# Cross-attention maxima over pairs of 512-key chunks, in bursts of one 512-column round

## The reference

```
x = x + cross_attention(layernorm(x), ctx)      # q: 512 x 512, ctx: 8192 x 512, 16 heads of 32, RoPE
x = x + self_attention(layernorm(x))            # causal, 512 x 512
x = x + experts(layernorm(x))                   # top 4 of 32 experts, and a shared one

cross_attention:  q = x @ W_q + b_q;  k, v = split(y @ W_kv + b_kv);  q, k = rope(q), rope(k)
                  softmax(q @ k.T / sqrt(32)) @ v, then @ W_o + b_o
```

## Time and profile before

| | |
|---|---|
| median of three runs | 1490.36 us |
| profiled execution | 1485.93 us, span 1484.6 us |
| busy, share of the span | PE 95%, DVE 78%, ACT 69%, POOL 42% |
| granted TensorE clock, mean | 0.988 |
| first score burst, last score burst | at 72.7 us, at 582.8 us |
| second, third, fourth stage begin | 590.5, 1147, 1265 us |

### The profile page before, as it was taken

One profiled execution on the slowest core, in us unless ns is written; L12 is line 12 of the kernel. 1 busy time (PEld: TensorE's weight loads), 2 busy tenths in 40 slices (PEclk: granted clock), 3 DMA queues, 4 the chain that ended last, 5 costly groups with the idle time before them and its releaser, 6 DMA issues.

```text
span 1484.6 us, 29090 instructions
## 1 busy us (share of the span) xinstructions
PE 1406.3 (95%) x11020; PEld 854.0 (58%) x11020; DVE 1150.7 (78%) x2814; ACT 1023.8 (69%) x1318; POOL 626.9 (42%) x426
## 2 busy tenths in 40 slices
PE   7999999999999976999999999999999899899993
PEld 5866666666666643555555555555555766644441
DVE  6888777877877775899999999998988866533334
ACT  5577777777777775988899888988998456301221
POOL 0199787877787982132122223220000311054541
PEclk9999999999999999999999999999999999999997
DMA  5464344444333326855545544556551240357994
GB/s 197 136 238 157 128 143 162 151 141 144 128 128 128 129 74 191 219 131 129 121 118 128 127 117 119 132 119 173 130 125 48 98 170 2 148 191 280 410 407 174
DMA packets 94592, 229.74 MB, mean 155 GB/s; under 512 B 12737, under 2 KB 13130, under 8 KB 91638
## 3 DMA queue, kind: packets, MB, share of 16 engines
q1 hardware_dynamic: 88288, 218.37, 46.8%
q0 software_dynamic: 5600, 8.42, 1.6%
q10 hardware_dynamic: 566, 1.09, 0.2%
HBM read 171.15 MB, written 64.91 MB: 159 GB/s over the span
## 4 chain that ended last, share of the span: by engine, by line
PE 68%; POOL 13%; DVE 7%; ACT 4%; issue 4%; DMA 3%; SPq 1%; POOLq 0%; ACTq 0%; DVEq 0%
PE PS L817 18%; PE PS L841 16%; PE PS L340 6%; PE PS L344 6%; PE PS L299 4%; PE PS L1648 4%; POOL kr L633 3%; POOL W_ L631 3%; POOL kr L630 3%; POOL R L622 2%; PE PS L1665 2%; PE PS L849 2%; PE PS L1607 2%; DVE rel L607 2%; POOL kl L648 1%
## 5 line engine op out<-in xcount | busy, mean ns | idle before, releaser
L875 ACT ACTIVATE P<-PS 128x1024 f32<-128x1024 f32 x512 | 487.2, 1027 | 63.6 <-PE PS L817 58.8
L607 DVE CUSTOM_DVE_ANT_0 rel<-PS,rel 128x256 f32<-128x256 f32 x1024 | 363.2, 420 | 106.2 <-PE PS L299 104.3
L935 DVE TENSOR_TENSOR W_<-W_,P 128x2048 f32<-128x2048 f32 x108 | 254.8, 2425 | 8.4 <-ACT P L875 8.1
L841 PE MATMUL PS<-P,qe 128*32 128x256 f32 (+1 forms) x4032 | 255.8, 386 | 0.0
L935 DVE TENSOR_TENSOR acc<-acc,P 128x2048 f32<-128x2048 f32 x108 | 245.3, 2335 | 12.8 <-ACT P L875 12.5
L841 PEld LDWEIGHTS PS<-P,qe 128*32 128x32 f32 x4032 | 115.5, 109 | 115.8 <-issue 54.5
L459 ACT ACTIVATE rel<-PS 128x1024 f32<-128x1024 f32 x128 | 131.6, 1028 | 71.8 <-PE PS L299 71.7
L344 PE MATMUL PS<-Wh,R 128*128 128x512 f32 x512 | 179.3, 413 | 0.0
L340 PE MATMUL PS<-R,Wh 128*128 128x512 f32 x512 | 175.8, 414 | 3.1 <-ACT kr L426 3.1
L465 ACT ACTIVATE rel<-PS 128x1024 f32<-128x1024 f32 x128 | 131.5, 1028 | 45.0 <-PE PS L299 44.4
L299 PE MATMUL PS<-khd,qh 32*128 32x256 f32 x2048 | 130.0, 327 | 23.8 <-DVE mpart L607 11.9
(11 more groups left out here) (304 smaller groups left out, 2061.8 us busy)
## 6 DMA issues: line engine op xcount, KB each, us to landing
khd<-kscr SPq DMA_DIRECT2D x129, 256.0 KB, 4.2
y<-in_y SPq DMA_DIRECT2D x16, 1024.0 KB, 5.2
vscr<-W_ SPq DMA_DIRECT2D x16, 1024.0 KB, 4.9
kscr<-khd SPq DMA_DIRECT2D x16, 1024.0 KB, 6.9
kscr<-kl SPq DMA_DIRECT2D x16, 1024.0 KB, 5.0
qe<-vscr SPq DMA_DIRECT2D x64, 256.0 KB, 2.7
kl<-kscr SPq DMA_DIRECT2D x63, 256.0 KB, 4.3
Wp<-in_w_e SPq DMA_DIRECT2D x6, 1536.0 KB
```

What stands on the lines that cost most here:

```text
L607: last = dve.tensor_tensor_reduce(out=rel[i][:, j, t, :], in0=PS[:, 2 * b + j, t * 256:(t + 1) * 256], in1=rel[i][:, j, t, :], scale=1.0, ...
L841: ins = pe.matmul(PS[32 * hd:32 * hd + 32, 6, cols], vt[n % 3][:, j, 32 * hd:32 * hd + 32], P[z % 4][:, hd, cols], start=kt == 0, stop=kt ...
L875: act.activation(P[s % 4][:, 2 * pr:2 * pr + 2, :], PS[:, 2 * b:2 * b + 2, :], ACT.Exp, scale=SCALE).then_inc(exp_done, 1)
L935: dve.tensor_tensor(a[:, :, :], a[:, :, :], P[s % 4][:, :, :], ALU.add).then_inc(summed, 1)
```

## The change

In the first stage a chunk is no longer folded in itself. Key i of chunk 2m is paired with key i of chunk 2m+1, `kd` = key of 2m − key of 2m+1 (512 columns), and `b` is chunk 2m+1. There are 8 pairs of chunks, and for each 4 groups, 4 query tiles and 2 pairs of heads: 256 half steps. `half_step(k)` is one burst of four matmuls of 512 columns, in the order `kh`, `kd`, `kh`, `kd`: the `b` scores of half step k into banks 0 and 1 or 2 and 3, and the differences of half step k+1 into banks 4 and 5. ACT's relu for k+1 follows; DVE's two instructions of 512 columns for k need the relu taken one half step before. PE waits at half step k for that relu of k (`relued`, k+1) and for DVE to have finished k−2 (`max_taken`, k−1). One `kd` and one `kh[1]` serve all pairs, so POOL and ACT wait before they overwrite a group (`last_b`), and ACT waits before it overwrites `kr[0]` until POOL has made the difference from it.

The table `SCORES` starts at slot 216 (before: 170), advances by 5 and 6 in turn, by 5 from k = 192 on, and skips to 936, 1128 and 1320 for the pairs 4, 5 and 6, whose keys are ready then. The last half step has slot 1640, 104 after the last unit; before it was 1540 at the latest. 21 of the half steps come after the last projection matmul. `ROPE`, `KEY_HIGH`, `Y_HIGH`, `KEY_LOW`, `Y_LOW` stay where they were.

In the third stage the units with `u % 3 == 2` begin with a mask matmul of 384 columns for each head (zeros, mask, mask), and the scores of both tiles are added to it. ACT prepares the wider mask with three instructions in place of one.

```diff
-Y_HIGH, Y_LOW, KEY_LOW, SCORES_1, SCORES_2, MAXIMA = {}, {}, {}, {}, {}, {}
+Y_HIGH, Y_LOW, KEY_LOW, SCORES, MAXIMA = {}, {}, {}, {}, {}
...
+KEYS_READY = {(c_, g_): slot_ + 8 for slot_, (c_, g_) in KEY_HIGH.items()}
+slot_ = 0
+for k_ in range(-1, HALF_STEPS):
+    m_, g_, t_, h_ = step_of(min(k_ + 1, HALF_STEPS - 1))
+    slot_ = max(slot_ + (6 if k_ % 2 and k_ < 6 * 32 else 5), KEYS_READY[2 * m_ + 1, g_])
+    SCORES[slot_] = k_
...
-    def score_pairs(n, which, left, right):
-        c, g, qp = n // 8, n % 8 // 2, n % 2
-        for t in range(2):
-            qt = 2 * qp + t
-            for hd in range(4):
-                rows = slice(32 * hd, 32 * hd + 32)
-                keys = slice(256, 512) if hd // 2 == which else slice(512, 768)
-                o = PS[:, 2 * (left if hd // 2 == which else right) + hd % 2, t * 256:(t + 1) * 256]
-                last = pe.matmul(o, qh[rows, g, qt * 128:(qt + 1) * 128], khd[c % 2][rows, g, keys],
+    def half_step(k):
+
+        for j in range(2):
+            if k >= 0:
+                m, g, qt, which = step_of(k)
+                rows = slice(32 * (2 * which + j), 32 * (2 * which + j) + 32)
+                last = pe.matmul(PS[:, 2 * (k % 2) + j, :], qh[rows, g, qt * 128:(qt + 1) * 128], kh[1][rows, g, :],
+                                 start=True, stop=True)
+            if k + 1 < HALF_STEPS:
+                m, g, qt, which = step_of(k + 1)
+                rows = slice(32 * (2 * which + j), 32 * (2 * which + j) + 32)
+                last = pe.matmul(PS[:, 4 + j, :], qh[rows, g, qt * 128:(qt + 1) * 128], kd[rows, g, :],
                                  start=True, stop=True)
...
+            if k < 0:
+                pe.wait_ge(q_out_ps, 4)
             else:
-                pe.wait_ge(q_out_ps, 4)
-            score_pairs(n, 0, n % 3, (n + 1) % 3).then_inc(sc1_made, 1)
...
+                pe.wait_ge(relued, k + 1)
+            if k > 1:
+                pe.wait_ge(max_taken, k - 1)
+            half_step(k).then_inc(sc_made, 1)
...
+        if slot in SCORES and SCORES[slot] + 1 < HALF_STEPS:
+            k = SCORES[slot] + 1
+            act.wait_ge(sc_made, scored(k - 1))
+            if k > 1:
+                act.wait_ge(max_taken, k - 1)
+            act.activation(rel[k % 2][:, :, :], PS[:, 4:6, :], ACT.Relu).then_inc(relued, 1)
...
-    def larger(n, hp, i, b):
-        c, g, qp = n // 8, n % 8 // 2, n % 2
+    def larger(k):
+        m, g, qt, which = step_of(k)
         for j in range(2):
-            for t in range(2):
-                last = dve.tensor_tensor_reduce(
-                    out=rel[i][:, j, t, :], in0=PS[:, 2 * b + j, t * 256:(t + 1) * 256], in1=rel[i][:, j, t, :],
-                    scale=1.0, scalar=NEG, op0=ALU.add, op1=ALU.max,
-                    accum_out=mpart[:, 4 * (2 * hp + j) + g, 2 * qp + t, c:c + 1])
+            last = dve.tensor_tensor_reduce(
+                out=rel[k % 2][:, j, :], in0=PS[:, 2 * (k % 2) + j, :], in1=rel[k % 2][:, j, :],
+                scale=1.0, scalar=NEG, op0=ALU.add, op1=ALU.max, accum_out=mpart[:, 4 * (2 * which + j) + g, qt, m:m + 1])
...
-                if c > 1 and g == 0:
-                    pool.wait_ge(sc2_made, 8 * (c - 1))
-                pool.wait_ge(k_turned, turned(c, g, 3))
-                pool.tensor_tensor(khd[c % 2][:, g, 512:768], x[:, 0:256], x[:, 256:512],
-                                   ALU.subtract).then_inc(k_turned, 1)
+                if c % 2:
+                    if c > 1:
+                        pool.wait_ge(sc_made, scored(last_b(c - 2, g)))
...
+                    pool.wait_ge(k_turned, turned(c, g, 3))
+                    pool.tensor_tensor(kd[:, g, :], kr[0][:, g, :], x, ALU.subtract).then_inc(k_turned, 1)
...
+        if u % 3 == 2:
+            for hd in (2 * hp, 2 * hp + 1):
+                pe.matmul(PS[:, 2 + hd, 0:384], idr[:, :], mkr[:, :], start=True, stop=False)
+            for qt, off in TILES[2]:
+                w = 128 * (qt + 1)
+                for hd in (2 * hp, 2 * hp + 1):
+                    ins = pe.matmul(PS[:, 2 + hd, off:off + w], qk[0][ROWS[hd], g, qt * 128:(qt + 1) * 128],
+                                    qk[1][ROWS[hd], g, 0:w], start=False, stop=qt == 0)
```

More of the change, by code:

```diff
@@ L60, with step_of @@
     KEY_LOW[12 * (first_key(c_) + 8 + {0: 5, 1: 6, 14: 1, 15: 1}.get(c_, late_)) + 5] = c_
[L61 to L69, removed]
+    if c_ == NCH - 2:
+        FIRST_KEYS = max(KEY_LOW) + 30
+HALF_STEPS = 2 * 16 * (NCH // 2)
+def step_of(k):
+    return k // 32, k % 32 // 8, k % 8 // 2, k % 2
+KEYS_READY = {(c_, g_): slot_ + 8 for slot_, (c_, g_) in KEY_HIGH.items()}
[4 more added lines that the diff above has]
+    SCORES[slot_] = k_
+    if k_ >= 7 * 32 and k_ % 8 == 7:
+        MAXIMA[slot_ + 2] = k_ % 32 // 8
 SECOND_KEYS = 12 * 8 * NCH + 2
 UNIT_SLOTS = 12 * len(UNITS)
-SLOTS = max(*SCORES_2, *MAXIMA, SECOND_KEYS) + 1
+SLOTS = max(*SCORES, *MAXIMA, SECOND_KEYS) + 1
 STEPS = 2 * 4 * 4 * NCH
@@ L211, in program @@
     Wl = sbt("Wl", [128, 4, 1024], F32R)
-    khd = [sbt(f"khd{i}", [128, 4, 768], F32R) for i in range(2)]
-    kh = [x_[:, :, 0:512] for x_ in khd]
+    kh = [sbt(f"kh{i}", [128, 4, 512], F32R) for i in range(2)]
+    kd = sbt("kd", [128, 4, 512], F32R)
     kl = sbt("kl", [128, 4, 512], F32R)
@@ L218, in program @@
     first, sb1 = stack()
-    mpart = sb1("mpart", [128, 16, 4, NCH])
+    mpart = sb1("mpart", [128, 16, 4, NCH // 2])
     qh = sb1("qh", [128, 4, 512], F32R)
     ql = sb1("ql", [128, 4, 512], F32R)
-    rel = [sb1(f"rel{i}", [128, 2, 2, 256]) for i in range(2)]
+    rel = [sb1(f"rel{i}", [128, 2, 512]) for i in range(2)]
     y = sb1("y0", [128, 4, 512])
@@ L268, in turned, with scored, last_b @@
     def turned(c, g, step):
-        return 4 * (4 * (c - 1) + g) + step
+        return 16 * (c // 2) + 12 * ((c - 1) // 2) + (3 + c % 2) * g + step
+    def scored(k):
+        return k + 2
+    def last_b(c, g):
+        return 32 * (c // 2) + 8 * g + 7
     def free_keys(c):
@@ L425, in first_act @@
                     act.wait_ge(kl_done, c - 1)
+                if c > 1 and c % 2 == 0:
+                    act.wait_ge(k_turned, turned(c - 1, u, 4))
                 act.activation(kr[c % 2][:, u, :], PS[:, 6 + n % 2, :], ACT.Identity,
@@ L471, in first_act_side @@
             else:
-                act.wait_ge(rope0, 4 * g + 3)
+                act.wait_ge(rope0, 3 * g + 3)
             if c > 1 and g == 0:
-                act.wait_ge(sc2_made, 8 * (c - 1))
                 act.wait_ge(kh_out[c % 2], 16 * (c // 2))
-            act.copy(khd[c % 2][:, g, 0:512], kr[c % 2][:, g, :]).then_inc(kh_done, 1)
+            if c > 2 and c % 2:
+                act.wait_ge(sc_made, scored(last_b(c - 2, g)))
+            act.copy(kh[c % 2][:, g, :], kr[c % 2][:, g, :]).then_inc(kh_done, 1)
         if slot in QUERY_HIGH:
@@ L800, in second_pe @@
     def second_pe():
-        pe.wait_ge(relu2, 8 * NCH)
+        pe.wait_ge(relued, HALF_STEPS)
         pe.wait_ge(nm_done, 4)
@@ L1243, in scores @@
             for hd in (2 * hp, 2 * hp + 1):
-                ins = pe.matmul(PS[:, 2 + hd, off + w - 128:off + w], idr[:, :], mkr[:, :], start=False, stop=True)
+                ins = pe.matmul(PS[:, 2 + hd, off + w - 128:off + w], idr[:, :], mkr[:, 128:256], start=False, stop=True)
         ins.then_inc(scored, 1)
@@ L1302, in third_act @@
         act.copy(idr[:, :], ident[:, :]).then_inc(vw_high, 1)
-        act.copy(mkr[:, :], mask[:, 0:128]).then_inc(vw_high, 1)
+        act.mul(mkr[:, 0:128], mask[:, 0:128], 0.0)
+        act.copy(mkr[:, 128:256], mask[:, 0:128])
+        act.copy(mkr[:, 256:384], mask[:, 0:128]).then_inc(vw_high, 1)
         for g in range(4):
```

84 lines of the change are left out of this document (29 added, 55 removed).

## The result

| | before | after |
|---|---|---|
| median | 1490.36 us | 1495.1 us (17 runs, 1493.0 to 1496.4) |
| after / before | | 1.0032, 95% interval 1.0025 to 1.0040 |
| span of the profiled execution | 1484.6 us | 1491.8 us |
| mean granted TensorE clock | 0.988 | 0.971 |
| busy in 73 to 583 us: PE, DVE, ACT, POOL | 486, 404, 382, 410 us | 490, 358, 373, 405 us |

What follows compares the result with a forecast made beforehand. First stage taken as bound by PE, with waits for DVE and DVE setting the pace in chunks 14 and 15; 28.4 (second stage earlier) + 0.5 (clock) + 1 (mask) = 29.9 us saved, forecast 1460 us, range 1450 to 1480.

Steps and rivals of the forecast that it cites:

- A burst: First stage, PE: one round instead of two takes 0.33 us, saving 0.11 us per burst, bounds none and 0.11.
- the first rival: First-stage bursts are no cheaper: five-slot intervals stay 1.79 us, six-slot ones go to 2.02; 18 us more, 1478; chance 0.12.
- The chain through ACT: First stage: each burst waits for the relu behind the one before, 1.74 us, which sets the five-slot intervals.
- DVE: First stage: a 512-column instruction takes 0.61 us, bounds 0.53 and 0.69; two fit in a half step, so DVE leaves the path.
- ACT's other work: First stage: copies of keys, values and contexts between relus make some intervals late, 4 us in all, bounds 0 and 9.
- The third rival: ACT becomes the first stage's bound, copies delaying relus by up to 0.5 us, and the kernel gets slower; chance 0.07.
- POOL: First stage: the longer first group costs PE about 1.2 us; otherwise nothing left on the path, under 2 us to spare.
- SP's transfers keep their slots and sizes: First stage: the forecast's statement on SP's DMA transfers, with no time added for them in the sum.
- The tail: Behind slot 1535: 21 bursts without projections, paced by the 1.74 us chain, 36.5 us; the second stage 2.3 us after the last.
- the second rival: The clock falls to 1.2 GHz while PE is thinly used behind the last projection: 7 us, 1467; chance 0.12.
- The gap behind the last burst: From the last burst to the second stage PE waits only for DVE, 2.3 us, the row-maxima transfers being done.
- The mask: Self-attention: one pair of mask matmuls goes, the other grows; 0.06 to 0.15 us in 8 places, 1 us, bounds 0 and 3.

Runs made afterwards that it cites:

- the last run: Half steps of the last pair four slots apart, a dummy in every slot behind the last unit, against the repaired kernel with its start on DVE: 1467.80 us.
- the run with the dense tail: Changed kernel with a dummy matmul in four of five slots behind the last unit, in place of one in three: 1489.03 us, ratio 0.9994.

## Why the prediction was wrong

In the order of its sum; the slots' times are given as forecast and as measured.

- **A burst** (0.33 in place of 0.44 us). Wrong, the costliest step. I split 0.44 evenly over two rounds because the loads went in two batches. The batches are real, but the second loads while the first round streams, so its 0.11 was hidden already. Measured 0.43. With 160 intervals 0.05 and 93 intervals 0.11 to 0.12 longer it is the 18 us of the first rival, which I had given 0.12. Its numbers, 1.79 and 2.02, are those measured. The second clause of the rule in the Trainium skill (TensorE: Matmul & The Clock Gate, Part 2, step-by-step: a load goes ahead if it targets the background buffer of weights) agrees with the runs: two rounds on the same rows take 0.44 us to the next projection, one round 0.43. No text of mine had a term for the change of shape, though rows 3 held it: 0.44 behind a burst of 0.22 us of columns.
- **The chain through ACT** (1.74 us). Right as a mechanism; it never decided in the middle, since PE needs 1.79. At full clock it is 1.64: the burst starts 0.05 us after the relu's end in the last run, where I took 0.15 from rows 9.
- **DVE**. Right: 0.62 us from start to start (596.68 to 597.30 us), and off the path. Its waits were the 0.07 us per burst up to slot 1320 that I had read from rows 7, 12 us in all, and another 8 from there to slot 1500; the other 6 us of the middle are bursts moved behind it.
- **ACT's other work** (4 us). Not seen in the middle: intervals stay at 1.79 and 2.02 with copies between the relus, as the longer PE part covers them. The third rival, ACT as the bound, did not come, although a sign like the one it was to have did: weight loads wait for ACT's relu 168 times, 85.8 us in all, while PE itself idles for it in 13 places.
- **POOL** (1.2 us at the start, "nothing left on the path"). Wrong. I counted what PE waits for, not that ACT now waits for POOL before it may overwrite `kr[0]`, a wait that the diff adds. Slot 216 came at 83.4 us, forecast 84.3; but slot 288 gives back 5 us. Slot 936: 337.7, forecast 320.9, of which 11 us are the burst and 6 the start.
- **Slot 936 to 1320**: 129.7 us, forecast 123.7, all of it the burst.
- **Slot 1320 to 1535**: 91.9 us, forecast 74.8. 11.6 us are PE's idle stretch. The step that failed is "SP's transfers keep their slots and sizes". Their order and sizes did stay (the first loads for the second stage went from slot 1483 to 1487); but a slot is an order, not a time. With the slots of these units 11% faster and POOL slower for odd chunks (5.3 us a group in place of 4.7), the wait of SP for POOL that stands ahead of the store grew into the path.
- **The tail** (21 bursts at full clock, and 2.3 us): 42.9 us measured from slot 1535, 42.8 forecast, and right only by chance: the clock fell (1.93 in place of 1.74, the second rival, 4 us), and ACT's 4 us, which I had added there, did not come. The step that failed is the argument against that rival: that the clock had stayed up at the old end with its short waits. There projections stood between the bursts.
- **The gap behind the last burst**: 2.3 us forecast, 2.57 measured. Right.
- **The mask** (1 us, bounds 0 and 3). Right in sign, mis-sized: 4.0 us. I priced columns and records, not the two changes of shape.

The balance: 28.4 us were forecast for the first stage and 11.7 lost, 40 us apart, of which about 20 are the burst (11, 6 and 3 by stretches), 5 the start, 12 the store (13 by the run that moved it), 3 or less not traced to one wait, among the last units; in the tail the clock's 4 us and the 4 not spent on ACT cancel. Between the stages 0.5 us was lost in place of won. The mask gave back 2.7 more than forecast, and a clock phase of 3.4 us near 1294 us that the new trace doesn't have gave 1.2 (the run with the dense tail has that phase again, and its last stage is as long as before). That leads from 29.9 us faster to 7.2 us slower in the span.

The forecast was built on one row (the split of 0.44 us) and three arguments that put a cost at nothing (POOL, SP's transfers, the clock of the tail). The range reached 1480 because I had taken the rivals one at a time, while two of them came together with two waits that were no rivals at all.

## What to carry to other kernels

When a stage gets faster, walk through each queue that did not get faster, and list what stands ahead of every transfer that someone waits for: here one wait and six loads ahead of a store cost almost half of what the change brought. Matmuls of different shape should be visited seldom and stayed with long: here merging two rounds within a visit brought nothing, and each visit more cost 0.43 to 0.44 us. And where a chain through another engine leaves TensorE thinly used for tens of microseconds, look at the granted clock and try filling the gaps with matmuls that nobody waits for.

## What the runs showed of the hardware

- A change of TensorE from 128-row matmuls to a group of 32-row ones and back costs 0.43 us beyond the columns: 0.10 ahead of the group, 0.22 behind its columns, 0.11 behind the first 128-row matmul. It was the same for groups of four and of eight matmuls. Within the group the loads of a second round on the same rows are hidden: a second round of 256 columns costs 0.12 us, its columns.
- DVE and POOL delayed each other when both read two operands from SBUF: 0.69 us became 4.61 and 5.09 us on DVE, 1.28 became 3.33 us on POOL. The maxima, with one operand in PSUM, kept their 0.62 us beside POOL's work. The Trainium skill states this (SBUF — State Buffer, Who interferes with whom: a VectorE instruction with two SBUF inputs contends with one of GpSimd that reads SBUF, and the shared ports are an exclusive lock). The traces agree: DVE's instruction of 66.80 us ended at 71.41, 0.5 us after POOL's of 66.26. I had not looked there, since no part of the change had both.
- With one burst and one or two dummies between bursts the granted clock fell to 1.2 GHz at 564.4 us, 5 us into the tail, and stayed there to the tail's end; with a burst and four dummies in 1.64 us it was at 2.4 GHz for the whole tail.
- A store of 1 MB took 8.6 us from issue to landing behind another of 1 MB and six loads, and 4.7 us as the first of its queue.
